# A fused vision-transformer block: the small steps of the main loop at new places in each engine's order

## What is computed

```python
h = _L0_tok_ref(x, L0_tok_W, L0_tok_b)              # patches @ W + b, then a class token in front
h = h + _L0_attn_ref(_layernorm(h, axis=-1), ...)   # the mixer
h = h + _L0_ffn_ref(_layernorm(h, axis=-1), ...)    # 8 experts, capacity 1.25
# the mixer:
xz = x @ W_in
x_inner, z = jnp.split(xz, 2, axis=-1)
x_conv = silu(conv1d(x_inner, conv_w) + conv_b)
Bm, Cm = jnp.split(x_conv @ W_x, 2, axis=-1)
delta = jax.nn.softplus(x_conv @ W_dt + b_dt)
def step(h, inp):
    x_t, d_t, B_t, C_t = inp
    A_disc = jnp.exp(d_t[:, :, None] * A)
    h = A_disc * h + (d_t * x_t)[:, :, None] * B_t[:, None, :]
    y_t = jnp.einsum('bds,bs->bd', h, C_t)
y = (ys + D * x_conv) * silu(z)
out = layernorm(y @ W_out) * gamma + beta
```

## Time and profile before

| | |
|---|---|
| median of 3 runs | 2841.7 us |
| lowest and highest | 2839.04 and 2841.87 us |
| profiled execution, span from first to last instruction | 2853.9 us |
| busy: PE, DVE, ACT, POOL | 2494.7, 2261.8, 2052.6, 2278.9 us |
| mean granted TensorE clock | 0.926 of full speed |

### The profile page before, as it was taken

How to read it: one execution, slowest core, us unless ns; L and a number is a source line. 1 busy time by engine, 2 the same in 40 slices (tenths; PEclk the granted TensorE clock), 3 DMA queues, 4 the chain that set the end, 5 groups by cost and what they waited for, 6 DMA issues and landing times.

```text
span 2853.9 us, 37922 instructions
## 1 busy us (share of the span) xinstructions
PE 2494.7 (87%) x12595; PEld 1565.8 (55%) x12595; DVE 2261.8 (79%) x2290; ACT 2052.6 (72%) x4500; POOL 2278.9 (80%) x1126
## 2 busy tenths in 40 slices
PE   7788889889888888889888989888885679999997
PEld 5444445445555445545454555544441467888886
DVE  2699999999999999999999999999999763222222
ACT  3688888888888888888888888888875433333342
POOL 0599999999999999999999999999998243444432
PEclk9899898999999999898989999999985789999999
DMA  3455544555444555554555544445542224666652
GB/s 104 110 131 130 119 111 111 135 129 116 112 111 111 128 122 124 127 118 111 120 122 132 117 113 111 111 116 125 127 106 48 84 90 167 209 212 205 217 185 88
DMA packets 165465, 361.08 MB, mean 127 GB/s; under 512 B 18353, under 2 KB 89593, under 8 KB 157848
## 3 DMA queue, kind: packets, MB, share of 16 engines
q1 hardware_dynamic: 152504, 329.59, 45.9%
q0 software_dynamic: 12768, 29.08, 3.2%
HBM read 293.86 MB, written 69.30 MB: 127 GB/s over the span
## 4 chain that ended last, share of the span: by engine, by line
PE 42%; DVE 24%; issue 13%; ACT 12%; POOL 7%; another core or an unknown queue 1%; DMA 0%; DVEq 0%; POOLq 0%; SPq 0%; ACTq 0%
DVE arena L1531 14%; PE banks L1403 7%; DVE arena L1520 5%; PE banks L1382 5%; PE banks L1037 5%; PE banks L1076 4%; PE banks L1058 4%; POOL arena L531 4%; PE banks L1108 4%; PE banks L1120 3%; ACT banks L724 3%; PE banks L1390 3%; ACT arena L731 2%; ACT L845 1%; POOL arena L622 1%
## 5 line engine op out<-in xcount | busy, mean ns | idle before, releaser
L1531 DVE TENSOR_TENSOR_SCAN arena<-banks,arena 128x788 f32<-128x788 f32 x768 | 1339.2, 1784 | 59.4 <-ACT banks L724 29.3
L531 POOL TENSOR_TENSOR arena<-arena 128x1576 f32<-128x1576 f32 x384 | 1247.2, 3259 | 18.3 <-ACT arena L803 14.4
L724 ACT ACTIVATE banks<-arena,neg_a 128x392 f32<-128x392 f32 x1536 | 838.9, 580 | 246.4 <-DVE arena L1531 242.7
L1520 DVE TENSOR_TENSOR arena<-arena,banks 128x1576 f32<-128x1576 f32 x320 | 570.0, 1781 | 43.4 <-issue 32.1
L1108 PE MATMUL banks<-arena,gather_q 128*32 128x394 f32 x3072 | 354.8, 536 | 91.5 <-POOL arena L531 91.2
L682 POOL DMA_INDIRECT out_tokens<-arena x114 | 114.8, 1007 | 265.7 <-DVE arena L1736 246.5
L1058 PE MATMUL banks<-arena,v_lo 128*128 128x394 f32 x768 | 311.9, 553 | 7.6 <-DVE logits L1550 4.5
L1721 DVE TENSOR_TENSOR arena<-banks,arena 128x384 f32<-128x384 f32 x57 | 31.8, 558 | 361.5 <-PE banks L1403 316.7
L1076 PE MATMUL banks<-arena,wdt 128*128 128x394 f32 x576 | 245.5, 579 | 37.4 <-ACT arena L845 37.4
L1037 PE MATMUL banks<-wtok,arena 128*99 128x192 f32 x1536 | 265.9, 331 | 11.2 <-DMA arena<-in_x 11.2
L1037 PEld LDWEIGHTS banks<-wtok,arena 128*99 128x99 f32 x1536 | 249.1, 168 | 42.7 <-issue 33.4
(11 more groups left out here) (249 smaller groups left out, 4157.7 us busy)
## 6 DMA issues: line engine op xcount, KB each, us to landing
arena<-delta_du_scratch SPq DMA_DIRECT2D x384, 394.0 KB, 10.5
arena<-in_w_pack SPq DMA_DIRECT2D x57, 1155.0 KB
delta_du_scratch<-arena SPq DMA_DIRECT2D x96, 394.0 KB, 3.2
arena<-in_x SPq DMA_DIRECT2D x32, 1176.0 KB, 11.8
rows_scratch<-arena SPq DMA_DIRECT2D x32, 297.0 KB
rows_scratch<-arena SPq DMA_DIRECT2D x32, 294.0 KB
arena<-in_b SPq DMA_DIRECT2D x57, 96.0 KB
arena<-in_conv_w SPq DMA_DIRECT2D x1, 2304.0 KB, 11.0
```

Source lines behind the costliest of these rows:

```text
L531: pool.tensor_tensor(v[:, :, :], v[:, :, :], c_rep[r][:, u % NG].unsqueeze(1).to_broadcast([P, NQ, N2]), ALU.mult).then_inc(s_mulp, 1)
L724: ins = act.activation(o, d, ACT.Exp, scale=neg_a[:, c:c + 1])
L1520: dve.tensor_tensor(hb[(UNITS * n + u) % BUFS][:, :, :], rep[m][:, :, 1, :], ps_b[:, 0:N2].unsqueeze(1).to_broadcast([P, NQ, N2]), ALU.mul ...
L1531: dve.tensor_tensor_scan(v, decay[k % 2], v, 0.0, ALU.mult, ALU.add).then_inc(s_scan, 1)
```

## The change

The change keeps every operation and its operands in the main loop and alters three things. First, nearly all small steps stand at other k or u on ACT, POOL, PE and DVE. Second, on DVE a product `bx` is no longer issued right before the scan that reads it, but a scan or more ahead (`bx(i, 1)` after scan 0, `bx(i, 2)` after scan 3 and so on), and `spread_b` on PE moves with it and waits for the product that used the bank before. Third, on ACT `silu_z(i)` moves from step 5 to step 12, and `exp_ln_tables()` from behind it to step 23. (`b_keep` becomes a list with one entry, and the arena grows by 100 columns; neither changes an instruction.)

```diff
-        K_OF = (20, 1, 21, 15, 6, 5, 4, 14, 12, 13)
-        MADE = (1, 3, 2, 10, 6, 5, 4, 9, 7, 8)
+        K_OF = (20, 1, 21, 17, 6, 7, 5, 13, 10, 15)
+        MADE = (1, 3, 2, 10, 5, 6, 4, 8, 7, 9)
...
@@ ACT, body @@
-                    if 1 in on and k == 5:
-                        silu_x(i + 1, o)
-                    if 0 in on and k == 5:
-                        copy_c(i, r, r, 3)
-                    if 0 in on and k == 5:
-                        silu_z(i, r)
-                        exp_ln_tables()
+                    if 1 in on and k == 4:
+                        silu_x(i + 1, o)
+                    if 0 in on and k == 4:
+                        copy_c(i, r, r, 3)
+                    if -2 in on and k == 4:
+                        copy_back_t(i - 2, r, 0)
...
-                    if 1 in on and k == 11:
+                    if 1 in on and k == 10:
                         softplus_up(i + 1)
-                    if 1 in on and k == 11:
-                        softplus_t(i + 1)
-                    if -1 in on and k == 12:
+                    if -1 in on and k == 11:
                         copy_out(i - 1, r, 0)
-                    if 1 in on and k == 13:
+                    if 1 in on and k == 11:
+                        softplus_t(i + 1)
+                    if 1 in on and k == 12:
+                        copy_product(i + 1, o, r, Z + 1)
+                    if 0 in on and k == 12:
+                        silu_z(i, r)
+                    if 1 in on and k == 12:
                         softplus_ln(i + 1)
+                    if -1 in on and k == 13:
+                        copy_out(i - 1, r, 1)
+                    if -1 in on and k == 13:
+                        out_squares(i - 1, o)
...
+                    if k == 23 and (0 in on or 1 in on):
+                        exp_ln_tables()
@@ PE @@
             def spread_b(n, r, u):
                 if u == 0:
                     pe.wait_ge(s_bc3, n + 1)
-                need(pe, s_bx, bx_count(n, u))
-                if u == KEEP + 1:
-                    pe.wait_ge(s_bkeep, n + 1)
+                p = SPREAD[SPREAD.index(u) - 1]
+                m = n if u != SPREAD[0] else n - 1
+                if p not in BY_POOL:
+                    need(pe, s_bx, bx_count(m, p) + 1)
+                if p in KEPT:
+                    need(pe, s_bkeep, len(KEPT) * m + KEPT.index(p) + 1)
@@ DVE, body @@
-                    if 0 in on:
-                        if k % 2 == 0 and k // 2 not in BY_POOL:
-                            bx(i, k // 2)
-                        scan(i, k)
                     if -2 in on and k == 0:
                         row_stats(i - 2, r)
-                    if -1 in on and k == 5:
+                    if 0 in on and k == 0:
+                        bx(i, 0)
+                    if 0 in on:
+                        scan(i, k)
+                    if 0 in on and k == 0:
+                        bx(i, 1)
+                    if 0 in on and k == 3:
+                        bx(i, 2)
+                    if -1 in on and k == 3:
                         take_y(i - 1, o, 2)
+                    if 0 in on and k == 4:
+                        bx(i, 3)
+                    if 0 in on and k == 7:
+                        bx(i, 4)
...
```

More of the change, by code:

```diff
@@ L68 @@
 UNITS = MB * NG
-KEEP = 1
 BY_POOL = (5, 9)
+KEPT = (1,)
 BXS = UNITS - len(BY_POOL)
+SPREAD = tuple(u for u in range(UNITS) if u not in BY_POOL or u in KEPT)
 BUFS = 5
-LAG = 3
 REP = 16 * SP
@@ L80 @@
 FIRST, LAST = slice(0, COLS - 8), slice(COLS - 8, COLS)
-ARENA = 43800
+ARENA = 43900
 W_HI = FF + FF // 2
@@ L86, in need @@
 def need(eng, sem, count):
-    if not isinstance(count, int) or count > 0:
+    if count > 0:
         eng.wait_ge(sem, count)
@@ L648, in body @@
                             router_consts()
+                    if 0 in on and u == 2:
+                        fill_rows(i, r)
+                    if 0 in on and u == 2:
+                        bx_pool(i, 5)
+                    if 1 in on and u == 4:
+                        softplus_sum(i + 1)
                     if 1 in on and u == 5:
@@ L651, in body @@
                     if 1 in on and u == 6:
+                        make_delta(i + 1)
+                    if -1 in on and u == 6:
+                        rstd_out(i - 1)
+                    if 1 in on and u == 6:
                         make_du(i + 1, o)
-                    if -1 in on and u == 8:
-                        rstd_out(i - 1)
+                    if 0 in on and u == 6:
+                        bx_pool(i, 9)
+                    if 2 in on and u == 6:
+                        rstd_front(i + 2)
                     if -1 in on and u == 9:
                         apply_gamma(i - 1)
-                    if -1 in on and u == 10:
+                    if 1 in on and u == 9:
+                        last_bc(i + 1, o)
+                    if -1 in on and u == 9:
                         add_residual(i - 1, o)
@@ L1177, in body @@
                         spread_c(i, r, r, 2)
-                    if 0 in on and u == 1:
+                    if 0 in on and u == 0:
+                        spread_b(i, r, 2)
+                    if -1 in on and u == 1:
+                        state_sum(i - 1, o, 10)
+                    if -1 in on and u == 2:
+                        state_sum(i - 1, o, 11)
+                    if 0 in on and u == 2:
                         if 1 in on:
@@ L1183, in body @@
                         spread_c(i, r, r, 3)
-                    if 1 in on and u == 2:
+                    if 0 in on and u == 2:
+                        spread_b(i, r, 3)
+                    if -2 in on and u == 2:
+                        if i == PAIRS + 1:
+                            rank(FIRST, 1)
                         if 0 in on:
@@ L1293, in body @@
+                    if 1 in on and u == 11:
+                        spread_b(i + 1, o, 0)
+                    if 2 in on and u == 11:
+                        pe.wait_ge(s_trf_copied, 2 * (i + 2) + 2)
                         conv(i + 2, r, r, 2)
@@ L1640, in body @@
                         take_logits(i - 2, r)
+                    if 1 in on and k == 20:
+                        rest_bc(i + 1, o, r)
+                    if 0 in on and k == 20:
+                        take_y(i, r, 1)
+                    if 0 in on and k == 21:
+                        bx(i, 11)
             for i in range(-2, PAIRS + 2):
```

305 lines of the change are left out of this document (154 added, 151 removed).

## The result

The changed kernel took 2888.4 us (2888.1 to 2888.7, 4 runs) against 2840.6 us (2839.0 to 2841.9, 4 runs) for the kernel before: a ratio of 1.0174, 95% interval 1.016 to 1.0187, 47.8 us slower. The forecast was 2886 us and a range of 2850 to 2935.

A forecast was written before the change was run, and what follows sets the result against it. DVE and POOL were taken as nearly full, with ACT's stretch adding a stall: 62.43 + 3.7 + 0.4 = 66.5, plus 1.0 slow clock, 67.5 us per iteration; 1.44 more times 31 is 45 us: 2886 us, range 2850 to 2935.

The forecast's parts named there:

- The stretch on ACT: ACT's path from scan 8's end to decays 14, with three loads: 16.5 us against DVE's 12.8, so 3.7 us stall per iteration.
- Six loads at 1283 ns: ACT's table loads per iteration go from two to six; four more at 1.38 us each add 5.5 us of work.
- The drain of 1.38 us: Documented extra cost of each table switch on ACT; would put the time near 3013 us; chance 2 in 100.
- ACT's idle time for scans: ACT's waiting for scans per iteration was to fall from 7.0 to about 3 us.
- Scan 5: Around silu_x and its two loads at ACT's step 4, a DVE stall of 0.4 us in place of 0.31.
- The early products: On DVE, nine of ten products stand a scan ahead, each saving 0.18 us: 1.6 us per iteration.
- The slow-clock share: Time per iteration from late TensorE products at its lower clock: 1.70 us before, taken as 1.0, bounds 0 and 3.4.
- the prediction's lower bound: Slow-clock share of 0, since spread_b(0) behind a convolution, the 2.54 us wait, is needed about 1.5 us later.
- An idle time of some 2 us at unit 6: POOL waits for the squares at rstd_out; 63.5 us becomes 65.5, under the 66.5 us iteration, so nothing is counted.
- ACT's 7.0 us of idle time covers the loads: Rival: ACT's slack takes the loads in and POOL bounds the loop: 48 us less, 2793 us; chance 0.12.
- The low clock costing more: Rival: PE idles longer and products for delta come late; 2.5 us, iteration 69.0, 2933 us; chance 0.20.

The follow-up runs named there:

- e1: The changed kernel with the exp and ln load moved from step 23 to behind silu of z at step 12, four loads per iteration: 2876.6 us, ratio 1.0076.
- e2: The changed kernel with silu of z back beside silu of x at step 4, two loads per iteration: 2811.2 us, ratio 0.9847.
- e3: The kernel before with only ACT's silu of z and logarithm moved to step 12 and the load to step 23: 3013.6 us, ratio 1.0547.
- e7: The changed kernel with apply_gamma on POOL cut from 192 to 8 columns of each row: 2897.2 us, ratio 1.015.
- e8: The changed kernel with both silus at step 4, copy_back_t moved to step 5 and out_norm to step 20 on ACT: 2800.8 us, ratio 0.9813.

## Why the prediction was right

*The stretch on ACT.* Predicted were 3.7 us of waiting, some 2.5 ahead of scan 13. The rows have 2.50 and 1.12, together 3.62 (2.74 and 1.12 in most iterations). From the start of scan 8 (929.71) to that of scan 14 (948.10) it took 18.39 us; the path of 16.5 us from scan 8's end and the 1.77 us of the scan make 18.3. e1, e2 and e3 take a load out, all out, and put them into the old order, and the waits follow: 1.07, none, 4.55 us. This step is shown.

*Six loads at 1283 ns, 1.3 us from start to start.* As predicted; the load at 937.75 starts right behind the copy, and the logarithm and silu 0.01 to 0.02 us behind theirs. The drain of 1.38 us that the prediction gave 2 in 100 did not appear in a row of three loads either.

*ACT's idle time for scans.* Predicted to fall from 7.0 to about 3 us per iteration, measured 1.8. ACT is busy 5.3 us longer, as its sum had it, and idle 5.2 less.

*Scan 5.* Predicted 0.4 us, measured 0.17 without a disturbance.

*The early products.* Here the prediction miscounted. It said nine of ten stand a scan ahead, and so does the account of the change above. The products of units 0, 4 and 11 still stand right before the scan that reads them (the 1.87 us rows above), so it is seven, one of them, unit 2's, with a `take_y` between. The gain is 7 x 0.18 = 1.26, not 1.6 us. The price for each, 0.18, was right. With 0.36 more for DVE and 0.2 less at scan 5, the sum for an undisturbed iteration is 66.6 to 66.7 us instead of 66.5, and 66.87 was measured. The sentence above that each product now has a scan between it and its reader holds for the stretch from scan 8 to scan 14, which is all that the sum of ACT's stretch needs.

*The slow-clock share.* Taken at 1.0 us, measured 67.41 - 66.87 = 0.54 by the loads and 0.7 by the scans. The 2.54 us at the first product are gone, as the prediction's lower bound had it; instead scan 7 waits about 0.65 us where a product for delta comes late (its decays stand behind ACT's copy of it). The prediction named these products as the more sensitive ones. Just ahead of such a wait and in the same place of the iteration before, where scan 7 did not wait, the windows are:

```profile
988.00:990.00 2.00, 2.00 (x10) 0.84 (x3) 1.83 (x2) 1.99 (x4) 2.00 (x2) 0.51 1.07 163
```

```profile
921.00:923.00 2.00, 2.00 (x7) 1.15 (x8) 1.83 (x2) 1.99 (x4) 2.00 (x2) 1.00 1.08 170
```

It is so throughout this profile: in the 25 iterations with a wait at scan 7 the granted clock is at its lower level somewhere in the last 5 us ahead of scan 5, and in the six without one it never is. The mean clock did not change, 0.94 in both windows of the loop.

So this term was too large by 0.3 to 0.5 us, and the sum for the undisturbed iteration too small by 0.34, of which the miscount makes 0.36, scan 5 takes 0.2 off, and some 0.2 stay open: 67.5 us came out against 67.41 because two errors nearly cancelled. The time within 3 us of the forecast owes something to that.

*POOL.* An idle time of some 2 us at unit 6 that costs nothing was predicted. It is 3.1 us, and e7 shows that it costs nothing.

*The rivals.* That ACT's 7.0 us of idle time covers the loads is refuted by e3, where they would have had it all. The low clock costing more did not happen in the changed kernel; in e1 the waits that go with it grew.

## What to carry to other kernels

Idle time of an engine covers added work only as far as its buffers let it run ahead: ACT had 7.0 us idle per iteration against 5.3 us of added loads, and still made DVE wait 3.6 us, since three loads stood between two deadlines. Work out the path from release to deadline in each stretch, not the sum per iteration. Here the two silus in one place per iteration needed two loads and apart six, so functions of one table set are best kept together, and the compiled order, which shows the loads, is to be read before a step is moved. And where one PSUM bank is handed back and forth, the producer's and the consumer's places are one decision: moving one side alone cost 46 to some 330 us. Last, a difference of 10 us between two versions is to be looked for in the part that was edited: here it lay behind the loop.

## What the runs showed of the hardware

A scan whose input the instruction before it wrote starts 1.87 us after that instruction, and one that does not read it 1.69 us: the wait for the own result is 0.18 us in each of the rows seen. A table load between two activations costs 1.30 us from start to start (940.25 to 941.55), three in a row as well. The same program is not always equally long behind its loop: 636.1 and 651.4 us in two executions of the changed kernel, of which the part from the first to the last of the experts' stores is 446.3 and 455.4. The kernel before took 2839 to 2842 us in the first comparison, 2841 to 2852 in the last and 2850 to 2863 in the others; the effect of e7, and what seems one of e8 against e2, are smaller than this.
